# Quantised attentions taken by two sequences at a time: over themselves, then over the context, and the last experts' ends spread over four units

## The reference, cut to what matters

```python
def _fq(x, delta, zp, n_bits):
    xi = _round_ste(x / delta) + zp
    xq = jnp.clip(xi, 0.0, 2.0 ** n_bits - 1.0)
    return (xq - zp) * delta

def _attn(x, ctx, wq, wk, wv, wo, bo, dq, dk, dv, dw):
    ...                                  # q, k, v: 16 heads of 8 features
    sim = jnp.einsum('bhid,bhjd->bhij', _fq(q, dq, 128.0, 8), _fq(k, dk, 128.0, 8)) * SCALE
    attn = jax.nn.softmax(sim, axis=-1)
    out = jnp.einsum('bhij,bhjd->bhid', _fq(attn, dw, 0.0, 8), _fq(v, dv, 128.0, 8))
    ...
    return out @ wo + bo
h1 = _ln(x, ln1_g, ln1_b)
x = _attn(h1, h1, ...) + x               # over the sequence itself: 512 keys
h2 = _ln(x, ln2_g, ln2_b)
x = _attn(h2, context, ...) + x          # over the context: 154 keys
```

## Time and profile before

| | before |
|---|---|
| median of three runs | 1636.1 us |
| the profiled execution, device time | 1633.61 us |
| its span on the core (first to last instruction) | 1631.8 us |
| busy: PE, DVE, ACT, POOL | 71%, 68%, 55%, 42% of the span |
| the quantised stage, first to last step | 745.1 to 1215.6 us |
| TensorE's mean granted clock over the span | 0.825 |

### The profile page before, as it was taken

One profiled execution on the slowest core, in us unless ns is written; L12 is line 12 of the kernel. 1 busy time (PEld: TensorE's weight loads), 2 busy tenths in 40 slices (PEclk: granted clock), 3 DMA queues, 4 the chain that ended last, 5 costly groups with the idle time before them and its releaser, 6 DMA issues.

```text
span 1631.8 us, 27753 instructions
## 1 busy us (share of the span) xinstructions
PE 1165.1 (71%) x8832; PEld 676.5 (41%) x8832; DVE 1109.7 (68%) x3127; ACT 903.4 (55%) x2546; POOL 677.9 (42%) x1048
## 2 busy tenths in 40 slices
PE   2689999999978789684435354444438778888888
PEld 1355555555544448682111111122215444553545
DVE  2466776777667756277989899977764666666533
ACT  0344455555544346347767778888882254545542
POOL 5201110110111142545888878877771245344320
PEclk9899999999989999896555555555558899999999
DMA  5322341121072211216645557665560112111000
GB/s 160 69 49 55 64 139 36 43 73 35 17 150 48 46 45 46 80 46 162 120 95 111 100 108 123 119 106 107 106 108 10 26 38 55 28 33 48 1 1 26
DMA packets 263825, 115.53 MB, mean 71 GB/s; under 512 B 215928, under 2 KB 252672, under 8 KB 261504
## 3 DMA queue, kind: packets, MB, share of 16 engines
q1 hardware_dynamic: 258720, 107.34, 31.2%
q0 software_dynamic: 2048, 4.20, 0.9%
q10 hardware_dynamic: 2912, 2.22, 0.5%
HBM read 38.54 MB, written 16.45 MB: 34 GB/s over the span
## 4 chain that ended last, share of the span: by engine, by line
PE 39%; POOL 19%; DVE 15%; issue 15%; ACT 8%; DMA 2%; SPq 1%; another core or an unknown queue 0%; POOLq 0%; ACTq 0%; DVEq 0%
POOL arena L2236 10%; ACT arena L1536 5%; PE acc L1151 3%; PE trans L1124 3%; PE trans L1128 3%; POOL inv_total L2225 2%; PE misc L988 2%; PE misc L994 2%; PE score L1098 2%; PE trans L1275 2%; PE score L1090 2%; DVE minus_top L1927 2%; POOL arena L2183 2%; PE score L1287 2%; PE score L1289 2%
## 5 line engine op out<-in xcount | busy, mean ns | idle before, releaser
L2236 POOL TENSOR_SCALAR arena<-arena,inv_total 128x512 f16<-128x512 f32 (+1 forms) x512 | 299.6, 585 | 57.3 <-DVE inv_total L2003 16.4
L1927 DVE TENSOR_REDUCE minus_top<-score 128x4 f32<-128x616 f32 (+4 forms) x256 | 204.2, 804 | 150.9 <-PE score L1094 61.2
L2099 POOL TENSOR_TENSOR rstd<-spread,minus_half 128x4 f32<-128x4 f32 x36 | 37.6, 1044 | 534.0 <-DVE spread L1617 464.6
L1536 ACT ACTIVATE arena<-score,minus_top,exp_scale 128x512 f32<-128x512 f32 (+1 forms) x340 | 210.4, 625 | 17.5 <-POOL arena L2236 7.5
L1483 ACT ACTIVATE arena<-trans 128x512 f32<-128x512 f32 x240 | 140.5, 597 | 119.1 <-PE trans L1128 113.3
L1574 ACT ACTIVATE arena<-arena,minus_top 128x154 f32<-128x154 f32 x256 | 105.1, 412 | 131.8 <-DVE minus_top L2068 131.7
L1232 PE MATMUL score<-arena 32*128 32x512 bf16 (+1 forms) x340 | 68.4, 455 | 144.2 <-ACT arena L1536 143.1
L2009 DVE TENSOR_REDUCE top_score<-score 128x2 f32<-128x1024 f32 (+1 forms) x128 | 135.7, 1060 | 0.6 <-PE score L1232 0.5
L2256 POOL TENSOR_TENSOR arena<-arena,inv_total 128x512 f32<-128x512 f32 x64 | 66.5, 1040 | 144.7 <-DVE inv_total L2076 130.9
L1128 PE MATMUL trans<-arena 128*128 128x512 bf16 (+3 forms) x384 | 123.3, 330 | 0.0
L1536 ACT ACTIVATE arena<-trans,minus_top,exp_scale 128x154 f32<-128x154 f32 (+1 forms) x172 | 105.5, 620 | 16.3 <-POOL arena L2236 11.7
(11 more groups left out here) (283 smaller groups left out, 3075.7 us busy)
## 6 DMA issues: line engine op xcount, KB each, us to landing
arena<-q_terms SPq DMA_DIRECT2D x176, 64.0 KB
late<-arena SPq DMA_DIRECT2D x128, 64.0 KB, 2.0
q_terms<-arena SPq DMA_DIRECT2D x36, 128.0 KB
late<-k_terms SPq DMA_DIRECT2D x64, 64.0 KB
arena<-arena SPq DMA_TRANSPOSE x192, 3.1
by_expert<-zeros SPq DMA_DIRECT2D x2, 1472.0 KB, 9.8
arena<-by_expert SPq DMA_DIRECT2D x10, 256.0 KB, 2.9
from_expert<-arena SPq DMA_DIRECT2D x10, 256.0 KB
```

The lines of the kernel that those rows point to most:

```text
L1536: ins = nc.scalar.activation(probs[:, i % 3, j, of], quant_score[i % 3][:, j, of], ACT.Exp, bias=minus_top[:, at_col:at_col + 1], scale=ex ...
L1927: nc.vector.tensor_reduce(dst, src, axis=AX.X, op=ALU.max, negate=True).then_inc(top_ready, 1)
L2236: ins = nc.gpsimd.tensor_scalar(codes[:, (i - 1) % CODE_SOURCES, j, to], probs[:, (i - 1) % 3, j, of], inv_total[:, at_col:at_col + 1], HA ...
```

## The change: another order of units, other slots for the items

The units are run as 16, 17, 20, 21, 18, 19, 22, 23: two sequences over themselves, then the same two over the context, then the other two. What was found by a unit's number is now found by its place in this list. W, M, H of the unit before go to slots 9, 11, 13 of every unit (before: 10, 12, 13 in self units, 10, 12, 14 in cross units). In cross units K, V, Q of the next unit go to slots 8, 11, 14 (before: Q, K, V to 8, 9, 11). Unit 14 ends in slots 0 to 7 of unit 20 and unit 15 in slots 0 to 7 of unit 21. The gathers of unit 15 go to slots 5, 12, 19, 26 of unit 17 and 0, 3, 6, 9 of unit 20. Nothing is added or removed: every engine has the same instructions in the stage.

```diff
+QUANT_UNITS = [16, 17, 20, 21, 18, 19, 22, 23]
+QUANT_PLACE = {u: n for n, u in enumerate(QUANT_UNITS)}
...
-    for u in QUANT_UNITS:
-        f, per = QUANT_BASE[u], QUANT_BASE[u + 1] - QUANT_BASE[u]
-        if u == 16:
-
-            for v in (14, 15):
-                first = QUANT_BASE[v + 2]
-                for n in range(2 * TILES):
-                    at(quant, first + 5 + 3 * n, ("g", v, n))
-                for slot, name in ((0, "M4a"), (2, "M4b"), (4, "M5a"), (6, "M5b"), (8, "H")):
-                    at(quant, QUANT_BASE[v + 3] + slot, (name, v))
-        else:
-            for slot, name in zip((10, 12, 14) if per == 16 else (10, 12, 13), "WMH"):
-                at(quant, f + slot, (name, u - 1))
-        if u + 1 in QUANT_UNITS:
-            for slot, name in zip((8, 9, 11) if per == 16 else (15, 18, 22), "QKV"):
-                at(quant, f + slot, (name, u + 1))
+    for k, u in enumerate(QUANT_UNITS):
+        f, per = QUANT_BASE[u], QUANT_END[u] - QUANT_BASE[u]
+        if k:
+            for slot, name in zip((9, 11, 13), "WMH"):
+                at(quant, f + slot, (name, QUANT_UNITS[k - 1]))
+        if k + 1 < len(QUANT_UNITS):
+
+            for slot, name in zip((14, 8, 11) if per == 16 else (15, 18, 22), "QKV"):
+                at(quant, f + slot, (name, QUANT_UNITS[k + 1]))
+
+    for n in range(2 * TILES):
+        at(quant, QUANT_BASE[16] + 5 + 3 * n, ("g", 14, n))
+        at(quant, QUANT_BASE[17] + 5 + 7 * n if n < 4 else QUANT_BASE[20] + 3 * (n - 4), ("g", 15, n))
+    for v, u in ((14, 20), (15, 21)):
+        for slot, name in ((0, "M4a"), (2, "M4b"), (4, "M5a"), (6, "M5b"), (7, "H")):
+            at(quant, QUANT_BASE[u] + slot, (name, v))
```

## The result

The changed kernel is slower: a median of 1667.8 us (four runs, 1657.6 to 1680.0) against 1640.6 us for the kernel before (four runs, 1633.7 to 1648.7), a ratio of 1.015 with a 95% interval of 1.0095 to 1.020. The direction was forecast, the size was not: a net of +14.8 us and a time of 1650 us were predicted. The median lies 18 us above that time and 6 us above 1662, the top of the range.

The account below looks back on a forecast made before the run. It took DVE as nearly full in self units and held to ACT's pace each step in cross units. Self units -20.4 and cross units +35.2 gave net +14.8 us, forecast 1650 us, range 1636 to 1662.

Parts of the forecast that it names:

- (g to i): Waits for W, M and Q in cross units, 7.0 us: +4.7 each in units 20 to 22, -0.5 in 23.
- (g): W in slot 9 of cross units: its product is no longer covered, DVE waits 2.3 us; unit 23 was bare before.
- (c): W a slot earlier in self units 17 to 19: gross loss 1.0 us each, half caught up, +1.5 in all.
- (d): An expert's ending in slots 0 to 7 of units 20 and 21: 23.7 us against 18.5, +5.2 each.
- (a): Self units 17 and 18 lose one expert's ending each, 9.3 us apiece: -18.6.
- (b): Unit 17: four gathers leave, -2.5 us, and making codes for a cross unit saves a further 0.8.
- (i): Q one step behind H in cross units: DVE idles 3.9 us before Q.
- (e): Four gathers on POOL in unit 20 delay deviations, products and codes: +3.9 us, bounds 0 and 5.1.
- (f): K one step behind an expert's H: DVE waits 2.2 us in unit 20 and 3.6 in unit 21.
- taken in: Rival: cross units absorb the items in DVE's spare time; net -12.5 us, time 1624; chance 0.10.
- half as long: Rival: waits for K and Q behind H halve, 8.8 us less; net +6, time 1642; chance 0.20.
- POOL as the bound: Rival: POOL bounds units 20 and 21, its delays adding to endings and gathers; time 1660 us; chance 0.13.

Follow-up runs that it names:

- order_only: Changed kernel with the experts' endings put back into units 17 and 18 and all of unit 15's gathers into 17; quantised stage 493.8 us, ratio 1.014.
- gathers_back: Changed kernel with all gathers of unit 15 in unit 17, none in unit 20; quantised stage 494.1 us, against 494.2 in the changed kernel.
- slots_only: Kernel before, in its old unit order with its endings and gathers, given the changed W, M, H and K, V, Q slots; stage 489.7 us, ratio 1.014.
- k_later: Changed kernel with K of the next unit in slot 10 of a cross unit instead of 8; quantised stage 487.7 us, against 494.2.
- new_best: Changed kernel, its order and endings in cross units kept, with items set apart in other slots; quantised stage 466.5 us, ratio 0.9975 to the kernel before.

## Why the prediction was right in direction and short in size

The mechanism, waits on DVE that ACT then pays for, is what the traces show. The failed steps are terms of the sum, each sized too small: what is given back of the waits of W, M and Q in cross units (g to i), W in unit 23 (g), W in self units (c), the experts' endings (d) and the order of the units, which was costed at +0.7 us. In order, with what was measured:

- **(a), (b), self units win the endings and half of the gathers.** Right. From order_only to the changed kernel, unit 18 fell by 9.7 us (82.6 to 72.9), 9.3 predicted, and unit 17 by 11.9, for which 9.3 + 2.5 was predicted; four gathers in unit 17 are worth 3.3 us (gathers_back), 2.5 predicted. The 0.8 us for shorter codes in unit 17 did not come.
- **(c), W in slot 9 of a self unit: too small by 1.3 us.** The wait is 2.2 us now (1.28 in the earlier trace rows), as walked through, but I took half of the loss as caught up: 0.5 us in each of three units, 1.5 in all. In slots_only units 17, 18 and 19 lost 0.0, 1.4 and 1.4, 2.8 in all. Unit 17 got the whole back, because M's wait shrank there; units 18 and 19 got nothing back, and lost more than the 1.0 of the added wait. Why they did is open.
- **(d), the endings in cross units: the waits right, the sum too small by some 1.5 us a unit.** All three waits were predicted within 0.2 us in unit 21. From order_only to the changed kernel, unit 21 grew by 9.8 us, of which K's wait behind H is 3.1 (k_later); some 6.7 remain for the ending, 5.2 predicted. Unit 20 grew by 12.0; less 2.3 for K and 3.1 for the gathers there remain 6.6. Half of the error is in the base. The walk gave 23.7 us for slots 0 to 7 and the trace of unit 21 has 24.1, but I subtracted 18.5, which holds a long first step that (i) books once more as shortened; without the ending these slots take 17.8 us with the new slots (order_only).
- **(e), gathers in unit 20.** 3.1 us, 3.9 predicted.
- **(f), K behind H.** 2.3 and 3.1 us, 2.2 and 3.6 predicted.
- **(g) to (i), W, M and Q in cross units: too small by 3.0 us.** The waits were named rightly (2.23, 0.91 and 3.3 us; 7.0 in sum predicted, 6.4 measured). But I then took off 2.3 us a unit: 1.3 as falling on idle time that slots 12 to 15 had anyway, 1.0 as coming back in the next unit. In unit 22 of slots_only, slots 8 to 15 grew by 5.95 us (21.75 to 27.70), so only 0.5 of the 6.4 fell on idle time. There was not more to fall on: in these slots of unit 21 before, DVE's waits for ACT were 0.64 and 0.49 us, and one of 0.63 is still there. In slots 0 to 7 of the next unit 0.8 came back. Units 20, 21 and 22 lost 5.9, 5.2 and 5.2 us, where 4.7 each was predicted. In unit 23, W was not bare before, as I had it: DVE waited 1.07 us for its product in slot 10, and waits 2.23 in slot 9, and the unit lost 0.3 us where a gain of 0.5 was predicted.
- **The order: too small by 3.4 us, the largest single error, and mostly open.** It was costed at +0.7 (-0.8 for the codes in unit 17 and +1.5 for K in unit 21) and is +4.1. K is +1.3, about as predicted. Unit 17 became 1.0 us longer and not 0.8 shorter, and units 19, 20 and 22 together 1.7 us longer, for which nothing was booked. No run tests why.

In sum: slots 15.1 predicted and 19.3 measured; order 0.7 and 4.1; the experts' move -1.0 and +0.4. That is 14.8 against 23.8 us, 9.0 short. In the move, errors of both signs met: (d) was some 3 us too small, the gains and (e) and (f) made up for half of that.

The rest of the distance to the median is not in the mechanism. I added 2.5 us from the profiled execution to the median, by the three runs shown. With one more run the median before is 7.0 us above that execution, and the changed kernel's is 10.3 above its own. That is 7.8 of the 18 us; with 2.5 us added to the changed kernel's own execution the time would have been 1660, inside the range. The ratio of 1.0148 agrees with 1657.55 / 1633.61 = 1.0147.

Two of the signs need a word. The stretches outside the stage moved by 2.7 and 2.5 us, which the prediction had named as a sign of being wrong. It was a bad sign: over the twelve profiles the stage begins anywhere from 739.3 to 753.9 us, with the same code ahead of it. The others came out for the prediction: units 17, 18, 20, 21 and 22 at 75.4, 72.9, 58.3, 56.5 and 45.8 us, and a granted clock of 0.50 in units 20 and 21.

Of the rivals, "taken in" and "half as long" are refuted by the waits in unit 20, which are nearly as long as walked through. POOL as the bound did not happen either, though its net of 24.2 us and its 1660 come nearest to what was measured, by chance: it had the endings at 9.3 us each and the gathers at 5.1, where 6.6 to 6.7 and 3.1 were measured, and POOL is busy for 42.5 of the 58.3 us in unit 20, where 47 was reckoned. The Trainium skill's advice to interleave regimes with different most-contended engines (Perfetto Trace Analysis, section Optimization Strategy) finds no support here: order and move together cost 4.5 us by the chain of three kernels, and with items set apart the interleaved order stays behind. But what was interleaved here are whole units, not steps, so the advice in its full sense was not tried.

## What to carry to other kernels

In a pipeline of in-order engines with one or two steps of lead, ask of each side item first how many steps it stands behind what it needs and behind the next long item, and only then which engine has spare time on average. Here moving three items by one slot each gave back 17.5 us, while moving the experts' endings, which freed 21.6 us in units 17 and 18, came to +0.4 net. The waits that were walked through from the durations of their parts came out within 0.6 us, where no gather stood before them on POOL; of the 2.3 us a unit that were taken off them as caught up, 1.3 came. Look in the trace for the idle time that such an allowance is to fall on, and count it once.

## What the runs showed of the hardware beyond that

DVE's copy of codes, one instruction on the same 1024 columns, took 0.41 us in one step of unit 18 and 1.07 us in another, in which it began during POOL's work on two full operands. The rows of the kernel before, DVE's and then POOL's:

```profile
913.74 0.41 DVE L1992 TENSOR_SCALAR arena<-arena 128x1024 bf16<-128x1024 f16 x1
...
920.41 1.07 DVE L1992 TENSOR_SCALAR arena<-arena 128x1024 bf16<-128x1024 f16 x1
```

```profile
919.92 1.26 POOL L2160 TENSOR_TENSOR x<-normed,rows 128x512 f32<-128x512 f32 x1
```

POOL's instruction ends at 921.18 us and the copy at 921.48, 0.3 us later. Six of the stage's 192 copies took over 1 us; each of them began inside such an instruction (L2160 or L2103) and ended 0.28 or 0.29 us after it. The Trainium skill (SBUF — State Buffer, section SBUF: two separate sides) says that DVE in its two-port modes and GpSimd take turns on a shared pair of ports and block each other for a whole instruction; these six agree with that, without proving it.

Outside the stage, the twelve profiled executions differ by up to 20 us (1158.8 to 1179.2) without a change in the code there. In the last 196 us of new_best the granted clock is 0.93, and it took 8.9 us more than the same part of before at 0.99:

```profile
1450.00:1645.70 195.70, 169.66 (x968) 99.09 (x966) 92.47 (x425) 82.66 (x297) 54.92 (x73) 0.93 0.07 17
```

```profile
1445.00:1631.80 186.80, 160.57 (x970) 96.21 (x970) 92.62 (x426) 84.11 (x303) 55.86 (x75) 0.99 0.07 19
```

That is half of the 17.8 us by which the two differ outside the stage. Nearly all of the other half lies ahead of the stage, which begins at 753.9 and 745.1 us, and there the granted clock is no lower in new_best (0.92 in both from 500 us on). So the clock goes with a part of this scatter and not with all of it; there is one profile of each kernel, and no run shows what scatters the times of one kernel. It is the reason why the stage, read from the profile, tells more here than a single time.
